# Layer 0's fill: pair 1's x loaded early into the residual's buffer, pair 0's convolutions run between the mixing rounds

## What is computed

```
for i, typ in enumerate(('same', 'upsample', 'same', 'downsample')):
    s = style @ mod_w[i].T + mod_b[i]                       # per sample, per input channel
    weight = SCALE * w[i] * s[:, None, :, None]
    weight = weight * rsqrt(sum(weight * weight, axis=(2, 3)) + EPS)[:, :, None, None]
    out = conv_typ(out, weight) + bias[i]                   # 3 taps, 64 to 64 channels, a blur with the up and down steps
```

## Time and profile before

| what | value |
|---|---|
| median of 3 runs | 2025.45 us (2023.22 to 2029.68) |
| the profiled execution | 2025.23 us, span 2023.5 us |
| TensorE, VectorE, ScalarE busy | 1849.3, 883.8, 655.7 us |
| mean granted TensorE clock | 0.941 |

### The profile page before, as it was taken

How to read it: one execution, slowest core, us unless ns; L and a number is a source line. 1 busy time by engine, 2 the same in 40 slices (tenths; PEclk the granted TensorE clock), 3 DMA queues, 4 the chain that set the end, 5 groups by cost and what they waited for, 6 DMA issues and landing times.

```text
span 2023.5 us, 28675 instructions
## 1 busy us (share of the span) xinstructions
PE 1849.3 (91%) x9736; PEld 1534.3 (76%) x9736; DVE 883.8 (44%) x2607; ACT 655.7 (32%) x1203; POOL 96.0 (5%) x172
## 2 busy tenths in 40 slices
PE   5799999769999999985899999999879999999995
PEld 4677777558888888864688888888767888888873
DVE  5155555633433433344444444444563333333327
ACT  2355554323332333214322223322143333322310
POOL 2000000000000000000000000000000000001000
PEclk9699999869999999987899999999989999999986
DMA  6556656223332232335222222222233222222217
GB/s 123 118 140 158 150 145 148 77 59 77 75 86 65 77 86 75 78 52 120 60 71 56 72 57 68 70 60 61 57 118 67 77 76 76 75 71 68 62 41 311
DMA packets 229833, 181.30 MB, mean 90 GB/s; under 512 B 178648, under 2 KB 189944, under 8 KB 229534
## 3 DMA queue, kind: packets, MB, share of 16 engines
q1 hardware_dynamic: 222142, 173.35, 33.9%
q0 software_dynamic: 5008, 2.14, 0.9%
q10 hardware_dynamic: 2640, 5.26, 0.9%
HBM read 108.34 MB, written 42.99 MB: 75 GB/s over the span
## 4 chain that ended last, share of the span: by engine, by line
PE 75%; issue 9%; DVE 6%; SPq 4%; DMA 3%; ACT 2%; POOL 0%; POOLq 0%; ACTq 0%; DVEq 0%
PE ps L863 61%; PE ps L1560 4%; SPq L1140 4%; PE ps L956 3%; DMA filt<-filt 2%; PE ps L1004 2%; DVE w_lo L1313 1%; PE ps L947 1%; DVE filt L699 1%; PE ps L1580 1%; DVE x_last L1715 0%; POOL limes_rep L1640 0%; DMA nat_b<-in_L_ffn_lora_B 0%; ACT filt L404 0%; DMA raw<-in_x 0%
## 5 line engine op out<-in xcount | busy, mean ns | idle before, releaser
L863 PE MATMUL ps<-xp_hi,filt 128*128 128x512 f32 x1024 | 333.2, 407 | 15.2 <-DMA filt<-filt 13.0
L863 PE MATMUL ps<-w_hi,y_hi 128*128 128x512 f32 x768 | 314.6, 410 | 0.0
L863 PE MATMUL ps<-w_hi,y_lo 128*128 128x512 f32 x768 | 307.5, 400 | 0.0
L863 PE MATMUL ps<-w_lo,y_hi 128*128 128x512 f32 x768 | 307.2, 400 | 0.0
L863 PEld LDWEIGHTS ps<-xp_hi,filt 128*128 128x128 f32 x1024 | 188.3, 191 | 57.3 <-DMA filt<-filt 15.4
L688 DVE SCALAR_TENSOR_TENSOR xp_lo<-ps,mods_pair,xp_hi 128x512 fp32r<-128x512 f32 x128 | 96.2, 752 | 278.6 <-ACT xp_hi L394 278.6
L394 ACT ACTIVATE xp_hi<-ps,mods_pair 128x512 fp32r<-128x512 f32 x128 | 88.4, 690 | 368.5 <-PE ps L863 368.5
L863 PE MATMUL ps<-xp_lo,filt 128*128 128x512 f32 x512 | 203.4, 397 | 0.0
L410 ACT ACTIVATE y_nat<-ps,mods_pair 128x512 f32<-128x512 f32 x128 | 99.6, 778 | 246.2 <-PE ps L863 246.2
L863 PEld LDWEIGHTS ps<-w_lo,y_hi 128*128 128x128 f32 x768 | 146.7, 191 | 35.7
L863 PEld LDWEIGHTS ps<-w_hi,y_hi 128*128 128x128 f32 x768 | 148.3, 193 | 31.7
(11 more groups left out here) (325 smaller groups left out, 3128.2 us busy)
## 6 DMA issues: line engine op xcount, KB each, us to landing
x_in<-x_state SPq DMA_DIRECT2D x96, 256.0 KB, 3.9
x_res<-x_state SPq DMA_DIRECT2D x48, 512.0 KB, 4.0
x_state<-x_res SPq DMA_DIRECT2D x46, 512.0 KB, 2.9
filt<-filt SPq DMA_DIRECT2D x128, 128.0 KB, 2.7
filt<-filt SPq DMA_DIRECT2D x128, 96.0 KB, 2.4
raw<-in_x SPq DMA_DIRECT2D x16, 512.0 KB, 5.0
x_res<-in_x SPq DMA_DIRECT2D x16, 512.0 KB, 4.0
x_state<-raw SPq DMA_DIRECT2D x16, 512.0 KB, 3.0
```

What stands on the lines that cost most here:

```text
L863: ins = nc.tensor.matmul(out, st[x0], mv[x1], start=first and t == 0, stop=last and t == 2, **kw)
```

## The change

Three things change, all in layer 0's fill.

- Pair 1's x has a load of its own, issued directly behind pair 0's and ahead of the adapters, into `x_res` and with a semaphore of its own (`x1_loaded`). ACT and DVE split pair 1's x from there (`x_part`). SyncE waits for dve_x before the steps, so that the residual's load doesn't overwrite it.
- TensorE does no mixing round among pair 0's work. Rounds 0 and 1 come behind pair 1's halves, then pair 0's convolution of sample 0, rounds 2 and 3, the convolution of sample 1, pair 1's filter, rounds 4 to 7, and the transposes of `ffn_pe_prep`. ACT and DVE have their lists in the same order, with `ffn_act_prep` behind the rounds and `ffn_dve_prep` behind pair 1's filter.
- On SyncE the shifts of pair 1's filters go ahead of `mix_store`.

```diff
         def sp_load_x(sp, l, k):
+            if l == 0 and is_one(k):
+                for h in range(2):
+                    sp.dma_start(x_res[C * h:C * h + C, :, 0:L - h], x_conv[k][:, :, h:L]).then_inc(s["x1_loaded"], 16)
+                return
...
         def act_split_x(act, l, k, par):
+            if l == 0 and is_one(k):
+                act.wait_ge(s["x1_loaded"], 32)
+                act.sem_inc(s["x_loaded"], 32)
             act.wait_ge(s["x_loaded"], 32 * (pid(l, k) + 1))
...
+        def x_part(l, k, q):
+            return x_in[:, q] if l > 0 else (x_res if is_one(k) else x_nat)[:, q, 0:L - 1:2]
...
         def _(sp):
             sp_load_x(sp, 0, 0)
+            sp_load_x(sp, 0, 1)
             load_adapters(sp)
             ffn_load(sp, 0)
             for l in range(LAYERS):
                 if l > 0:
                     sp_load_x(sp, l, 0)
-                sp_load_x(sp, l, 1)
+                    sp_load_x(sp, l, 1)
                 sp_shift_filter(sp, l, 0)
                 sp_load_x(sp, l, 2)
+                sp_shift_filter(sp, l, 1)
                 if l == 0:
                     mix_store(sp)
-                sp_shift_filter(sp, l, 1)
...
+                if l == 0:
+                    sp.wait_ge(s["dve_x"], 2 * pid(0, 2))
                 with sp.Fori(0, GROUPS - 2) as i:
...
         def _(act):
                 for q in range(2):
                     act_first(act, l, 0, q, 0)
-                    if l == 0:
-                        mix_act(act, 2 * q)
-                        mix_act(act, 2 * q + 1)
                 act_filter(act, l, 0, 0)
-                if l == 0:
-                    mix_act(act, 4)
                 act_filter_in(act, l, 1, 1)
                 act_split_x(act, l, 1, 1)
                 act_halves(act, l, 1, 1)
                 if l == 0:
-                    for t in (5, 6, 7):
+                    mix_act(act, 0)
+                    mix_act(act, 1)
+                act_y(act, l, 0, 0, 0)
+                if l == 0:
+                    mix_act(act, 2)
+                    mix_act(act, 3)
+                act_y(act, l, 0, 1, 0)
+                act_filter(act, l, 1, 1)
+                if l == 0:
+                    for t in range(4, 8):
                         mix_act(act, t)
                     ffn_act_prep(act, 0)
...
         def _(dve):
                 dve_halves(dve, l, 1, 1)
-                if l == 0:
-                    ffn_dve_prep(dve, 0)
                 for q in range(2):
                     dve_y(dve, l, 0, 0, q, 0)
                 dve_filter(dve, l, 1, 1)
+                if l == 0:
+                    ffn_dve_prep(dve, 0)
...
         def _(pe):
                 pe_filter(pe, l, 0)
-                if l == 0:
-                    mix_pe(pe, 4)
                 pe_halves(pe, l, 1)
                 if l == 0:
-                    for t in (5, 6, 7):
+                    mix_pe(pe, 0)
+                    mix_pe(pe, 1)
+                    pe.wait_ge(s["dve_p"], smp(0, 0, 1))
+                    pe.wait_ge(s["dve_e"], edge_count(0, 0, EDGE_OPS))
+                    pe_conv(pe, 0, 0, 0)
+                    mix_pe(pe, 2)
+                    mix_pe(pe, 3)
+                    pe_conv(pe, 0, 0, 1)
+                    pe.wait_ge(s["dve_k"], smp(0, 0, 1))
+                    pe_filter(pe, 0, 1)
+                    for t in range(4, 8):
                         mix_pe(pe, t)
                     pe.wait_ge(s["mix_act"], 8)
-                    pe.wait_ge(s["dve_p"], smp(0, 0, 1))
-                    pe.wait_ge(s["dve_e"], edge_count(0, 0, EDGE_OPS))
+                    pe.wait_ge(s["act_y"], smp(0, 0, 1))
                     ffn_pe_prep(pe, 0)
...
                     pe.wait_ge(s["raw_dve"], part_count(0, 4))
```

More of the change, by code:

```diff
@@ L210, in build @@
         ps = ctx.enter_context(nc.psum_tensor("ps", [P, 8, 512], F32))
-        names = """first_loaded prep_loaded style_loaded ident_ready conv_forms forms_T forms_out s_pe sq_ready d_pe
+        names = """first_loaded x1_loaded prep_loaded style_loaded ident_ready conv_forms forms_T forms_out s_pe sq_ready d_pe
             var_ready std_ready bias_in bias_pe mods_ready pads_ready
@@ L243, in edge_count, with is_one @@
             return EDGE_OPS * (GROUPS * l + g) + step
+        def is_one(k):
+            return type(k) is int and k == 1
         def is_zero(k):
@@ L383, in act_split_x @@
             for q in range(2):
-                nc.scalar.activation(x_hi[:, q, 1:M + 1], x_part(l, q), ACT.Copy,
+                nc.scalar.activation(x_hi[:, q, 1:M + 1], x_part(l, k, q), ACT.Copy,
                                      scale=mods_pair[:, par, S0, q:q + 1]).then_inc(s["act_x"], 1)
-        def x_part(l, q):
-            return x_in[:, q] if l > 0 else x_nat[:, q, 0:L - 1:2]
+        def x_part(l, k, q):
+            return x_in[:, q] if l > 0 else (x_res if is_one(k) else x_nat)[:, q, 0:L - 1:2]
         def act_first(act, l, k, q, par):
@@ L681, in dve_split_x @@
                 dve.wait_ge(s["act_x"], smp(l, k, q))
-                nc.vector.scalar_tensor_tensor(x_lo[:, q, 1:M + 1], x_part(l, q), mods_pair[:, par, S0, q:q + 1],
+                nc.vector.scalar_tensor_tensor(x_lo[:, q, 1:M + 1], x_part(l, k, q), mods_pair[:, par, S0, q:q + 1],
                                                f(x_hi[:, q, 1:M + 1]), ALU.mult, ALU.subtract).then_inc(s["dve_x"], 1)
@@ L1873, in _ @@
                 if l == 0:
-                    for t in (5, 6, 7):
+                    mix_act(act, 0)
[8 more added lines that the diff above has]
+                    for t in range(4, 8):
                         mix_act(act, t)
                     ffn_act_prep(act, 0)
-                for q in range(2):
-                    act_y(act, l, 0, q, 0)
-                act_filter(act, l, 1, 1)
                 for q in range(2):
@@ L1962, in _ @@
                     pe_first(pe, l, 0, 0)
-                    if l == 0:
-                        mix_pe(pe, 0)
                     pe_edge(pe, l, 0, 3)
-                    if l == 0:
-                        mix_pe(pe, 1)
                     pe_first(pe, l, 0, 1)
-                    if l == 0:
-                        mix_pe(pe, 2)
                     pe_edge(pe, l, 0, 4)
-                    if l == 0:
-                        mix_pe(pe, 3)
                 else:
@@ L1981, in _ @@
                 pe_filter(pe, l, 0)
-                if l == 0:
-                    mix_pe(pe, 4)
                 pe_halves(pe, l, 1)
                 if l == 0:
-                    for t in (5, 6, 7):
+                    mix_pe(pe, 0)
[9 more added lines that the diff above has]
+                    for t in range(4, 8):
                         mix_pe(pe, t)
                     pe.wait_ge(s["mix_act"], 8)
-                    pe.wait_ge(s["dve_p"], smp(0, 0, 1))
-                    pe.wait_ge(s["dve_e"], edge_count(0, 0, EDGE_OPS))
+                    pe.wait_ge(s["act_y"], smp(0, 0, 1))
                     ffn_pe_prep(pe, 0)
-                pe.wait_ge(s["dve_k"], smp(l, 0, 1))
-                pe_filter(pe, l, 1)
-                if l == 0:
                     pe.wait_ge(s["raw_dve"], part_count(0, 4))
-                pe_conv(pe, l, 0, 0)
-                pe_conv(pe, l, 0, 1)
+                else:
+                    pe.wait_ge(s["dve_k"], smp(l, 0, 1))
+                    pe_filter(pe, l, 1)
+                    pe_conv(pe, l, 0, 0)
+                    pe_conv(pe, l, 0, 1)
                 pe_first(pe, l, 1, 0)
```

## The result

The changed kernel takes 2035.49 us (median of 10 runs, 2028.29 to 2039.02) against 2024.67 us (2021.5 to 2029.68, 10 runs) before: a ratio of 1.0052 with a 95% interval of 1.0039 to 1.0065, slower by 10.8 us. The forecast was 2032.5, and slower, by 7.1 us on the 2025.45 it started from; the time lies at the upper edge of its 2031 to 2035.5, the difference a little beyond its +10, and the range went to 2042. The profiled execution took 2039.02 us with a span of 2037.3, so it is one of the long ones; its span is 13.8 us over that of the kernel before, and 3 us of that is scatter of the two executions and not the change's.

A forecast was written before the change was run, and what follows sets the result against it. Layer 0's fill bounds: the chain through `ffn_load` behind the adapters. Pair 1's first convolutions +6.6 us and +0.6 behind make +7.2 on 2025.45: 2032.6, rounded to 2032.5; forecast 2031 to 2035.5, range 2018 to 2042.

The forecast's parts named there:

- The fill bounds, and what it gains or loses reaches the end: Layer 0's fill: TensorE is busy 91% of the span, so a microsecond saved or lost there moves the end equally.
- The filter shifts stay behind `ffn_load` and make TensorE wait some 12 us: Pair 0's shifts, issued at 66.6, let its first convolution start at 70.1; TensorE, through by 58, waits some 12 us.
- Rival A: Layer 0's fill: filter shifts landed when rounds 0 and 1 end at 56; 10.5 us faster, 2015; chance 0.13.
- The early x costs 5.0 us in front of `ffn_load`: SyncE's queue: pair 1's 1.05 MB ahead of the adapters cost 5.0 us, so `ffn_load` ends at 66.6.
- the upper bound of 7.8: Highest price of pair 1's early x ahead of the adapters: its whole landing, 7.8 us; the lower bound was 4.4.
- x on eight engines: Early x's transfer: on eight engines, not 16, it would cost an estimated 8.9 us, the sum 3.9 us more.
- TensorE's list from the convolution on: From 70.1, TensorE's convolutions, rounds, filter, transposes and evacuations in a row reach pair 1's first convolutions at 103.0, +6.6 us.
- C: Layer 0's fill: low clock, rounds 4 to 7 and transposes at half; +13.5 to +16, 2040; chance 0.17.
- the 5.5 and the 7.05 of the prediction: Layer 0's weight transposes: 7.05 us at the low clock, as in the sum; 5.5 at full clock, sum +5.6.
- The +0.6 behind it: Pair 1's first convolutions partly at half clock, +2.3 at most; the convolution behind may gain 1.7; together +0.6.
- The moves costed at nothing: `ffn_dve_prep`, `mix_store`, the kernel's and residual's loads (about 94), the dve_x wait and first edge loads: no cost.
- The signs named: Right: shifts issued at 65 to 68, 12 us gap ending at 70, pair 1's first convolutions at 101 to 105.

The follow-up runs named there:

- The order alone: The changed kernel with pair 1's x loaded as before, behind `ffn_load` into `x_nat`: 2033.34 us, ratio 1.0037.
- the kernel with x twice: The changed kernel loading pair 1's x a second time, into a free buffer, ahead of the adapters: 2037.40 us, ratio 1.0059.

## Why the prediction was right, and where it was off

1. *The fill bounds, and what it gains or loses reaches the end.* Held. The two profiles of each kernel put pair 1's first convolutions at 96.44 and 92.48 before, 105.37 and 106.12 after: 11.3 us apart on the average (8.9 in the first pair, 13.6 in the second), against 10.8 us in the times.

2. *The filter shifts stay behind `ffn_load` and make TensorE wait some 12 us.* Right in place and releaser: 12.03 us, ended by the shift. The order alone shows the same gap, and the shifts from ScalarE's queue give 8 us back. That the size came out is luck: the shifts landed 3.2 us later than forecast, and what TensorE does ahead of the gap ended later too, at 61.27 and not by 58. The forecast had rounds 0 and 1 at the full clock, 3.8 us; they took 6.92, at half, and began at 54.35, since pair 1's halves waited 3.33 us for VectorE until 52.26. Where the rounds ran faster and all else was alike up to there, in the kernel with x twice, the gap was 14.80 us. The clock ahead of the gap cost nothing at the end, since the shifts set when the convolution starts. Rival A (no wait left) came only in the kernels with adapter B behind the shifts.

3. *The early x costs 5.0 us in front of `ffn_load`.* This is the step that was mis-sized: `ffn_load` was put at 66.6 and ended at 69.59. The value taken was the bytes at the rate of 64 to 68; the average of the profiles is 8.3, over the upper bound of 7.8. The first convolution therefore started at 73.30 and not at 70.1. These 3.2 us, less 0.8 by which the list behind it was shorter, make 2.4 of the 3.7 us that the forecast of +7.1 lacks to +10.8 (the other 1.3 is within the scatter of the profiles). A reason seems near: the changed kernel moves 107 GB/s in 20 to 30, against 118. But the stretch doesn't hold the same traffic. Its packets, in the kernel before and then in the changed one:

```profile
20.00:30.00 10.00, 6.97 (x35) 5.52 (x35) 5.98 (x26) 2.04 (x8) 0.00 (x0) 1.00 0.55 107
...
DMA packets 104, 1.18 MB, mean 118 GB/s; under 512 B 16, under 2 KB 32, under 8 KB 32
...
DMA packets 653, 1.07 MB, mean 107 GB/s; under 512 B 553, under 2 KB 585, under 8 KB 592
```

The small packets (554 of them in the kernel before) went in 12 to 20 without x in front, and with x they fall into 20 to 30. In 30 to 50, where the packets are alike, the three profiles without x move 114 to 132 GB/s, mean 126, the six with one x 109 to 131, mean 119, and the one with two 118 and 130. So what x costs beyond its bytes is not settled. The 8.9 us worked out as an estimate for x on eight engines lies near the average, but the share in 12 to 20 was 1.09 with x, which speaks for sixteen.

4. *TensorE's list from the convolution on.* Predicted against measured: convolution 4.3 and 4.6, rounds 2 and 3 3.8 and 3.7, convolution 2.8 and 2.9, filter 1.9 and 1.8, rounds 4 to 7 7.6 and 7.25, evacuation 1.1 and 1.1, transposes 7.05 and 6.4, evacuation 4.35 and 4.37. Sum 32.9 and 32.1 us. Durations of like instructions carried over to within 0.4 us where the clock was the one assumed; the transposes, where it wasn't, came 0.65 us short.

5. *The clock.* The transposes began at the full clock (0.52 us a pair) and fell to half at 97.8 with TensorE at work, so they took 6.4, between the 5.5 and the 7.05 of the prediction:

```profile
97.23 0.39 PE L1333 MATMUL ps<-ident,raw 128*128 128x128 f32 x1
97.55 0.28 PE L1334 MATMUL ps<-ident,tail_raw 8*128 8x8 f32 x1
97.76 0.49 PE L1333 MATMUL ps<-ident,raw 128*128 128x128 f32 x1
98.18 0.28 PE L1334 MATMUL ps<-ident,tail_raw 8*128 8x8 f32 x1
```

The Trainium skill's page "TensorE: Matmul & The Clock Gate", section "Part 4: PE-mode transpose", says of transposes that they don't count as busy the way other matmuls do. The clearest rows on it are of the kernel with B behind the shifts and the transposes first: the transposes begin at 70.98 with no wait ahead, run at the full clock, and the first convolution directly behind them, at 76.19, is at half (0.78 us for its first matmul, 0.48 at the full clock). That agrees. It also stands against my reading of the earlier trace rows, where the clock rose among transposes that had other matmuls around them. But transposes are not the only thing it fell under: in the second profile of the changed kernel they ran at half from the first one on (0.49 us), after rounds at the full clock and 1.11 us idle. Rounds 4 to 7 kept the full clock in the changed kernel, so C did not come. Its slow rounds came in the kernel with B behind the shifts, where a wait of 7.39 us stood directly ahead of them.

6. *The +0.6 behind it.* Pair 1's first convolutions ran at half clock (5.5 us) and the next one at full: at 113.18 against 102.16 the distance was 11.0, up from 8.9, and 1.6 us of it came back in that convolution. That is +0.5 for the +0.6 predicted, and 9.4 us in the fill for the 7.2 of the sum.

7. *The moves costed at nothing.* The kernel's load and the residual's were issued at 97.54 and 100.50, later than the 94 of the prediction, but before the 102.99 of the earlier trace rows; no wait for them shows up to 140.

8. *The signs named.* ScalarE split pair 1's x at 51.61 with no wait for its load, and the gap was there with its releaser. The shifts were issued at 69.63 (65 to 68 was named), the gap ended at 73.3 (70), and the first convolutions started at 105.37 (101 to 105): all three are the step of item 3. The granted clock at the gap's end was to be 0.50; the view has 1.00 in 70 to 78, but the durations in 73.3 to 76.9 are those of half clock, as at 89.36 in the kernel before.

## What to carry to other kernels

A transfer that an engine's list now needs earlier must be looked for in its issuing queue, not at the time at which its source is ready: here the filters were ready at 51 and their DMA stood until 69.63 behind 58 us of blocked issues. Before a wait is filled with work from further down, ask which DMA that work needs and what is queued ahead of it. And when a wait is cleared, look at which load is late next: two edits, one of which gave nothing alone and the other 8.5 us, gave 21 us together, since one removed the wait and the other gave the remaining load its time.

## What the runs showed of the hardware beyond that

- An issue can block for 41 to 49 us: the second ffn_B piece did so behind 4 MB of adapters (41.06 us, 48.73 with x in front), and everything behind it in SyncE's queue with it; all eight pieces together took 49 to 51 us without x in front and 55 to 58 with it. With only adapter A in front, the eight pieces were through at 46.6.
- The adapters in pieces raised the share from 0.52 to 0.64 in 20 to 50 of the changed kernel to 0.98 to 1.01, but the rate only from 107 to 117 GB/s to 138 to 147.
- The granted clock of the view can be wrong: it stands at 1.00 in the changed kernel in 54 to 56, while two mixing rounds from 54.35 took 6.92 us, the half-clock duration. The durations are the safer reading.

```profile
54.00:56.00 2.00, 2.00 (x11) 2.00 (x10) 0.54 (x2) 0.84 (x2) 0.00 (x0) 1.00 0.52 116
```

- At the same place of the fill the clock differs between executions: the two rounds before the first convolution took 6.92 us here and 4.6 to 4.7 in the kernels with the shifts on ScalarE and with x twice, which are alike up to there. Only the gap behind them hid it.
